# Edge network: inverse deviations from a ScalarE square root and one VectorE reciprocal, in place of Newton steps on VectorE

## The chip, the cores and the metric

The kernel runs on one core of one Trainium2 chip. The metric is device time in microseconds (us). Before the change it is 17780.12 us, the median of 3 runs (17768.55 to 17810.48).

## The reference, cut to what matters

Four graph layers run one after another on 6250 nodes of 64 features and 206250 edges that are sorted by destination. The change is in the second one, the edge network with four heads. For head h and every edge:

```python
alpha = concat([q_i * K_v[src], q_i * K_E], axis=1) * scale   # 128 features
gate  = sigmoid(_ln(alpha, ln_g[h], ln_b[h]))
m     = concat([V_v[src], V_E], axis=1)
m     = (m @ Wu[h] + bu[h]) * gate
m     = leaky(_ln(m @ Wm[h] + bm[h], mln_g[h], mln_b[h]))     # 64 features
heads.append(segment_sum(m, dst))
```

where `_ln(x, g, b)` is `(x - mean) * rsqrt(var + 1e-5) * g + b` over the features. Each edge and head therefore needs two inverse deviations: one of alpha (128 features) and one of m @ Wm + bm (64 features).

## The kernel before, in words

Edges lie on the 128 partitions. A tile is 128 edges, a group is G = 4 tiles, and there are NG = 404 groups. With H = 4 heads a group has Q = G * H = 16 pairs of tile and head, so one step needs 16 inverse deviations of alpha and 16 of the output: a vector of 32 elements on each partition. Every stage over the edges is a loop over groups. The helper `steps` writes the first steps out, then a hardware loop whose body holds U = 4 groups, then the last steps.

The edge network's loop is `sweep1`, written once for each engine, as a pipeline in which step i works on several groups at a time:

- GpSimd gathers the rows of source and destination nodes (L1096), and for an older group multiplies and adds the affine vectors mg and mb (L1118, L1121).
- TensorE transposes the rows (L932), makes K_E (`edge_k`, L939), transposes the normalised alpha of group i-1 head by head (`turn`, L947), makes V @ Wu (`m_u`, L954), then of group i-2 the product with Wm (`o_pair`, L964 and L966), and of group i-4 the scatter by a one-hot matrix (`sums`, L977). The order is written out by hand: turn and m_u of heads 0 to 3, with edge_k, o_pair and sums between.
- ScalarE takes in step i, in this order: `norm` of head 1, sigmoid(0), norm of head 2, a copy, sigmoid(1), norm of head 3, sigmoid(2), take_o(0), sigmoid(3), norm(i, 0), take_o(1). `norm` (L781) is four ACTIVATEs with scale `rstd` and bias `shift`. `sigmoid(h)` (L787) waits for turn(h) and for gate_m(h - 2), since there are two gate buffers. `take_o` (L794, L795) squares and copies the output of o_pair.
- VectorE makes alpha (L550, and `edge_half` L523) and its statistics (L529). `gate_m(h)` (L535) multiplies the value by the gate of head h. Then comes the chain of small steps (L585 to L609), in which each `settle` waits for the step before it. Then the one-hot (L399), the normalised output y (L618), and `add` (L406), which adds the scattered sums to the accumulator; adds 0 and 1 take those of sums(0), adds 2 and 3 those of sums(1).

The chain holds 19 small steps (CH = 19). The first eight make the two variances, `var[0:16]` and `var[16:32]`. L600 makes a first guess of the inverse root by arithmetic on the bits, and L603, L605 and L607 refine it three times. L609 makes the shift. On VectorE gate_m(1) stands ahead of the chain and gate_m(2) behind it. On TensorE m_u(3) waits for gate_m(1), and sums(1) waits for adds 0 and 1. Everything on one engine is done in program order, and engines wait for each other by semaphores: chain1 counts the small steps, gated the sigmoids, gm_ready the gate_m, o_taken the take_o, normed the norms.

Elsewhere in the kernel square roots are made on ScalarE by the helper `root` (L761), followed by a reciprocal on VectorE (L367, L744).

Of the kernel before, what the change touches and what calls it, by code (L numbers as in the profile page):

```python
# [26 lines left out]
P = 128  # L27
# [26 lines left out]
MAGIC = float(0x5F3759DF)  # L54
# [21 lines left out]
def gnn(nc, a, out):  # L76
    ctx = ExitStack()
    with ctx:
# [126 lines left out]
        tmp = [view(2 * G * H, [2 * G * H]) for _ in range(5)]  # L205
# [73 lines left out]
        chain1 = sem("chain1")  # L279
        normed = sem("normed")  # L280
# [13 lines left out]
        CH = 19  # L294
# [44 lines left out]
        def _(dve):  # L339
# [166 lines left out]
            for s in range(2):  # L506
                link(V.memset(o_sq[s], 1.0), mark="sweep1")
# [5 lines left out]
            def sweep1(i, k, s, inside):  # L513
# [50 lines left out]
                if now[1]:  # L564
                    gate_m(1)
# [15 lines left out]
                var, u, d2, sm, m2 = tmp  # L581
                root = rstd[z]
                if now[2]:
                    dve.wait_ge(normed, Q * (i - 1))
                small_step(V.tensor_tensor(d2[:, 0:Q], st[:, :, 1], st[:, :, 4], ALU.subtract))  # L585
                small_step(V.tensor_tensor(sm[:, 0:Q], st[:, :, 1], st[:, :, 4], ALU.add))
                small_step(V.tensor_tensor(m2[:, 0:Q], st[:, :, 2], st[:, :, 5], ALU.add))
                small_step(V.tensor_reduce(var[:, Q:2 * Q], o_sq[odd], AX, ALU.add))  # L588
                settle()

                small_step(V.scalar_tensor_tensor(d2[:, 0:Q], d2[:, 0:Q], P / 4.0, d2[:, 0:Q],
                                                  ALU.mult, ALU.mult))
# [19 lines left out]
                if now[1]:  # L612
                    gate_m(2)
# [139 lines left out]
        def _(act):  # L753
# [18 lines left out]
            def sweep1(i, k, s, inside):  # L772
# [40 lines left out]
                if now[1]:  # L813
                    sigmoid(3)
# [3 lines left out]
                if now[2]:  # L818
                    take_o(1)
# [478 lines left out]
```

## Time and profile before

| | |
|---|---|
| median of 3 runs | 17780.12 us (17768.55 to 17810.48) |
| profiled execution | 17803.45 us |
| its span | 17801.3 us |
| mean granted TensorE clock | 0.738 |
| edge network's sweep, 2959 to 11520 us | 8561 us, 404 groups |
| PE busy in the sweep | 7228.05 us |
| DVE busy in the sweep | 7069.66 us |
| ACT busy in the sweep | 4760.21 us |
| POOL busy in the sweep | 5741.32 us |

The profile is of one execution. PE is TensorE, DVE VectorE, ACT ScalarE and POOL GpSimd. "Lnnn" is a line of the kernel before. A timeline's row gives the start in us, the duration in us, the engine, the line, the operation, its tiles, how many instructions are merged in the row, and in brackets the idle time before it with what ended it. The granted clock is a share of TensorE's full clock.

### The profile page before, as it was taken

The page shows a single profiled execution, that of the slowest core. Times are in us where ns is not written, and L with a number is a line of the kernel's source. Part 1 is how long each engine was busy: PE and PEld are TensorE (multiplying, and loading weights), DVE is VectorE, ACT ScalarE, POOL GpSimd, SP SyncE. Part 2 cuts the span into 40 slices and gives each one's busy share as a digit, 9 for nine tenths or more (in the row PEclk, how much of TensorE's full clock was granted, in tenths as well). Part 3 has the DMA queues.
Part 4 walks back from the last instruction along what each step waited for, and adds up shares of the span by engine and source line. Part 5 has one row for each costly group of instructions (what it writes and reads, how often), then busy time and mean ns, then how long its engine had stood idle before and what let it go on. Part 6 is the DMA issues. An engine that isn't in the chain of part 4 may idle for free.

```text
span 17801.3 us, 231614 instructions
## 1 busy us (share of the span) xinstructions
PE 11205.7 (63%) x52461; PEld 8279.5 (47%) x52462; DVE 10797.0 (61%) x29437; ACT 5021.6 (28%) x10532; POOL 10715.0 (60%) x10914
## 2 busy tenths in 40 slices
PE   5333335888888888888888888733333355555565
PEld 4222223666666565656566656522222233333454
DVE  7222225888888888888888888732222333333776
ACT  0000002555555555555555555400000011111000
POOL 0666664666666666666666666556666566666000
PEclk9999998888888888888888888755555555555555
DMA  0000002222222222222222222100000111111111
GB/s 25 22 22 22 22 22 70 62 63 64 61 62 63 64 62 62 62 62 62 62 62 62 62 63 64 42 22 22 22 22 22 29 46 46 46 46 46 51 48 40
DMA packets 474914, 838.02 MB, mean 47 GB/s; under 512 B 151155, under 2 KB 264980, under 8 KB 472725
## 3 DMA queue, kind: packets, MB, share of 16 engines
q0 software_dynamic: 310272, 637.61, 13.3%
q1 hardware_dynamic: 164116, 195.98, 3.6%
q14 instruction: 511, 4.19, 0.1%
q8 instruction: 15, 0.25, 0.0%
HBM read 755.78 MB, written 77.21 MB: 47 GB/s over the span
## 4 chain that ended last, share of the span: by engine, by line
DVE 30%; issue 27%; POOL 24%; PE 13%; DVEq 4%; POOLq 1%; ACT 1%; DMA 0%; SPq 0%; ACTq 0%
POOL arena L1096 22%; DVE acc L406 5%; DVE arena L529 4%; PE psum L977 4%; DVE arena L618 2%; DVE arena L588 2%; PE psum L939 2%; DVE arena L523 2%; PE psum L954 2%; DVE arena L561 2%; PE psum L947 2%; DVEq L329 1%; POOL idx_src L1103 1%; DVE arena L607 1%; DVE arena L603 1%
## 5 line engine op out<-in xcount | busy, mean ns | idle before, releaser
L1096 POOL DMA_INDIRECT arena<-table,idx_src x6464 | 6216.8, 962 | 4461.7 <-DVE arena L523 1803.1
L406 DVE TENSOR_TENSOR acc<-acc,psum 64x128 f32 (+2 forms) x6464 | 2041.1, 316 | 4230.0 <-PE psum L904 3019.2
L904 PE MATMUL psum<-arena 128*64 128x128 f32 x6464 | 1585.9, 427 | 3274.3 <-DMA arena<-table,idx_src 3274.3
L904 PEld LDWEIGHTS psum<-arena 128*64 128x64 f32 x6464 | 1266.1, 223 | 3593.9 <-issue 3569.1
L781 ACT ACTIVATE arena<-arena 128x128 f32<-128x128 f32 x6464 | 2648.8, 483 | 620.2 <-DVE arena L609 620.2
L1096 POOL DMA_INDIRECT arena<-table1q,idx_dst x1616 | 1873.1, 1159 | 492.3 <-issue 492.3
L787 ACT ACTIVATE arena<-psum,cols 128x512 f32<-128x512 f32 x1616 | 1256.1, 777 | 3047.8 <-PE psum L947 3044.6
L964 PEld LDWEIGHTS psum<-wm,arena 128*128 128x128 f32 x12928 | 1742.0, 202 | 560.2 <-issue 464.4
L954 PE MATMUL psum<-arena,wvu 128*128 128x512 f32 x3232 | 1966.9, 695 | 1.4 <-DVE arena L535 1.4
L964 PE MATMUL psum<-wm,arena 128*128 128x64 f32 x12928 | 1797.5, 285 | 0.1
L761 ACT ACTIVATE small<-small 128x49 f32<-128x49 f32 (+1 forms) x7 | 1.6, 233 | 6252.5 <-DVE small L365 3716.9
L977 PE MATMUL psum<-arena 128*128 128x128 f32 x6464 | 1140.3, 333 | 980.6 <-DVE acc L406 974.7
L977 PEld LDWEIGHTS psum<-arena 128*128 128x128 f32 x6464 | 1040.0, 237 | 1266.8 <-DVE acc L406 753.8
L939 PE MATMUL psum<-ke,arena 64*128 64x256 f32 x3232 | 1228.7, 514 | 341.3 <-DVE arena L523 341.3
L529 DVE BATCH_NORM_STATS2 arena<-arena 128x6 f32<-128x128 f32 x6464 | 1329.0, 279 | 118.6 <-DVE arena L523 45.3
L673 DVE TENSOR_TENSOR arena<-psum,arena 128x512 f32<-128x512 f32 x404 | 279.4, 692 | 1571.5 <-PE psum L1047 1571.5
L535 DVE SCALAR_TENSOR_TENSOR arena<-psum,cols,arena 128x512 f32<-128x512 f32 x1616 | 1198.9, 742 | 48.1 <-PE psum L954 43.7
L1121 POOL TENSOR_TENSOR arena<-arena,mb 128x1024 f32<-128x1024 f32 x404 | 1198.4, 2966 | 31.7
L947 PE MATMUL psum<-ident,arena 128*128 128x128 f32 x6464 | 1200.1, 315 | 5.7 <-ACT arena L781 5.7
L939 PEld LDWEIGHTS psum<-ke,arena 64*128 64x128 f32 x3232 | 722.5, 248 | 1015.3 <-DVE arena L523 608.3
L399 DVE TENSOR_TENSOR arena<-rel,iota_f 128x512 f32<-128x512 f32 x1616 | 1108.6, 686 | 96.4 <-issue 91.0
L1039 PE MATMUL psum<-ident,arena 128*64 128x128 f32 x1616 | 417.4, 414 | 1158.1 <-DMA arena<-table,idx_src 1158.1
(171 smaller groups left out, 14815.5 us busy)
## 6 DMA issues: line engine op xcount, KB each, us to landing
arena<-table,idx_src POOLq DMA_INDIRECT x6464, 2.4
kept_rows<-arena SPq DMA_DIRECT2D x404, 132.0 KB, 1.7
arena<-kept_rows SPq DMA_DIRECT2D x404, 132.0 KB, 2.1
arena<-in_edge_t SPq DMA_DIRECT2D x404, 128.0 KB, 2.8
arena<-table1q,idx_dst POOLq DMA_INDIRECT x1616
table<-arena SPq DMA_DIRECT2D x7, 1120.0 KB, 4.2
table1q<-arena SPq DMA_DIRECT2D x7, 896.0 KB, 6.4
table<-arena SPq DMA_DIRECT2D x2, 1568.0 KB, 5.1
```

The lines of the kernel that those rows point to most:

```text
L406: V.tensor_tensor(at_, at_, sums, ALU.add).then_inc(added, 1)
L529: V.bn_stats(st[:, n, :], alpha[z][:, n // H, n % H, :, :].rearrange("p a d -> p (a d)")).then_inc(stats1, 1)
L535: V.scalar_tensor_tensor(gm[odd][:, h, :, :].rearrange("p t n -> p (t n)"), psum[:, 4 + h % 2, :], cols[:, 0, h:h + 1], gate[:, h % 2, :], ...
L781: A.activation(at_, at_, ACT.Identity, bias=shift[z][:, n:n + 1], scale=rstd[z][:, n:n + 1]).then_inc(normed, 1)
L787: A.activation(gate[:, h % 2, :], psum[:, 2 + h % 2, :], ACT.Sigmoid, bias=cols[:, 2, h:h + 1], scale=cols[:, 1, h:h + 1]).then_inc(gated, 1)
L904: last = M.matmul(psum[0:D, z, t * WIN:(t + 1) * WIN], rows[s][:, t, :], onehot[z][:, t, :], start=True, stop=True)
L939: last = M.matmul(psum[:, 1, t * H * D:(t + 1) * H * D], xt[s][D:P, 2 * j + t, :], ke[D:P, :], start=True, stop=True)
L947: last = M.transpose(psum[:, 2 + h % 2, t * P:(t + 1) * P], alpha[odd][:, t, h, :, :].rearrange("p a d -> p (a d)"), ident[:, :])
L954: M.matmul(psum[:, 4 + h % 2, :], wvu[:, h, :], xt[prev].rearrange("p t n -> p (t n)"), start=True, stop=True).then_inc(m_done, 1)
L964: M.matmul(psum[:, 6, at_ + h * D:at_ + (h + 1) * D], gm[z][:, h, 2 * j + t, :], wm[:, h, :], start=h == 0, stop=False)
L977: last = M.matmul(psum[:, 7, at_:at_ + WIN], msg[z][:, t * H + 2 * half:t * H + 2 * half + 2, :].rearrange("p h d -> p (h d)"), onehot[z][ ...
L1096: K.indirect_dma_start(out=dst[:, t, :], out_offset=None, in_=table, in_offset=bass.IndirectOffsetOnAxis(ap=idx[:, t:t + 1], axis=0)).then ...
```

## The change

VectorE's chain loses the scaling of the variances, the first guess and the nine refining steps. The raw variances go to ScalarE, which makes their deviations by two ACTIVATEs with Sqrt (scale 1/128 and 1/64, bias from a new small tile `eps`), into a new tile `deviation`, and signals `rooted`. VectorE waits for that, takes one reciprocal of 32 elements, and makes the shift. The chain has 8 small steps now. gate_m(1) moves from ahead of the chain to behind its first six steps, gate_m(2) follows it, and both stand ahead of the wait for `rooted`. On ScalarE the square roots stand behind sigmoid(3), and take_o(1) moves from behind norm(i, 0) to ahead of it. Sigmoid and Sqrt are in different activation tables, so each step has two table loads.

```diff
-        tmp = [view(2 * G * H, [2 * G * H]) for _ in range(5)]
+        var, deviation = (view(2 * G * H, [2 * G * H]) for _ in range(2))
+        d2, sm, m2 = (view(G * H, [G * H]) for _ in range(3))
+        eps = view(2, [2])
...
-        CH = 19
+        CH = 8
...
+            link(V.memset(eps[:, 0:1], EPS1))
+            link(V.memset(eps[:, 1:2], EPS), mark="sweep1")
...
                 if now[0]:
                     edge_half(1)
-                if now[1]:
-                    gate_m(1)
...
+                small_step(V.tensor_tensor(d2, st[:, :, 1], st[:, :, 4], ALU.subtract))
+                small_step(V.tensor_tensor(sm, st[:, :, 1], st[:, :, 4], ALU.add))
+                small_step(V.tensor_tensor(m2, st[:, :, 2], st[:, :, 5], ALU.add))
+                after(dve, rooted, i)
+                small_step(V.tensor_reduce(var[:, Q:2 * Q], o_sq[odd], AX, ALU.add))
+                settle()
+                small_step(V.scalar_tensor_tensor(d2, d2, P / 4.0, d2, ALU.mult, ALU.mult))
+                settle()
+                small_step(V.tensor_tensor(var[:, 0:Q], d2, m2, ALU.add))
+                if now[1]:
+                    gate_m(1)
+                    gate_m(2)
                 if now[2]:
                     dve.wait_ge(normed, Q * (i - 1))
...
+                dve.wait_ge(rooted, i + 1)
+                small_step(V.reciprocal(root, deviation))
                 settle()
-                small_step(V.scalar_tensor_tensor(var[:, 0:Q], d2[:, 0:Q], P * EPS1, m2[:, 0:Q],
-                                                  ALU.add, ALU.add))
-                settle()
-                small_step(V.tensor_scalar(var[:, 0:Q], var[:, 0:Q], 1.0 / P, None, ALU.mult))
-                small_step(V.tensor_scalar(var[:, Q:2 * Q], var[:, Q:2 * Q], 1.0 / D, EPS, ALU.mult, ALU.add))
-                settle()
-                small_step(V.tensor_scalar(root.bitcast(I32), var.bitcast(I32), -0.5, MAGIC, ALU.mult, ALU.add))
-                for _ in range(3):
-                    settle()
-                    small_step(V.scalar_tensor_tensor(u, root, -0.5, root, ALU.mult, ALU.mult))
-                    settle()
-                    small_step(V.tensor_tensor(u, u, var, ALU.mult))
-                    settle()
-                    small_step(V.scalar_tensor_tensor(root, u, 1.5, root, ALU.add, ALU.mult))
-                settle()
-                small_step(V.scalar_tensor_tensor(shift[z], sm[:, 0:Q], -0.5, root[:, 0:Q], ALU.mult, ALU.mult))
-                if now[1]:
-                    gate_m(2)
+                small_step(V.scalar_tensor_tensor(shift[z], sm, -0.5, root[:, 0:Q], ALU.mult, ALU.mult))
+                settle()
...
                 if now[1]:
                     sigmoid(3)
+                act.wait_ge(chain1, CH * (i + 1) - 2)
+                Q = G * H
+                A.activation(deviation[:, 0:Q], var[:, 0:Q], ACT.Sqrt, bias=eps[:, 0:1], scale=1.0 / P)
+                A.activation(deviation[:, Q:2 * Q], var[:, Q:2 * Q], ACT.Sqrt, bias=eps[:, 1:2], scale=1.0 / D
+                             ).then_inc(rooted, 1)
+                if now[2]:
+                    take_o(1)
                 if now[0]:
                     act.wait_ge(chain1, CH * (i + 1))
                     norm(i, z, 0)
-                if now[2]:
-                    take_o(1)
-            steps(act, sweep1, NG, 4, 2)
+            steps(act, sweep1, NG, 4, 4)
```

## Rows read from the trace of the kernel before

**Rows 1.** The page, part 1: busy time, share of the span, instructions, by engine.
```profile
PE 11205.7 (63%) x52461; PEld 8279.5 (47%) x52462; DVE 10797.0 (61%) x29437; ACT 5021.6 (28%) x10532; POOL 10715.0 (60%) x10914
```

**Rows 2.** Windows, the edge network's sweep: length, busy by engine, clock, DMA share, GB/s.
```profile
2959.00:11520.00 8561.00, 7228.05 (x35549) 5153.79 (x35550) 7069.66 (x19872) 4760.21 (x10101) 5741.32 (x4840) 0.82 0.21 62
```

**Rows 3.** Waits in the sweep: total us, times, the longest; ACT, then PE.
```profile
ACT arena L787 <- PE psum L947: 3044.6, 1530, 5.8
ACT arena L781 <- DVE arena L609: 620.2, 298, 14.4
...
PE psum L977 <- DVE acc L406: 974.7, 364, 5.3
```

**Rows 4.** Timeline of DVE in the group at 6010 us.
```profile
6008.60 1.65 DVE L529 BATCH_NORM_STATS2 arena<-arena 128x6 f32<-128x128 f32 x8
6010.16 0.74 DVE L535 SCALAR_TENSOR_TENSOR arena<-psum,cols,arena 128x512 f32<-128x512 f32 x1
6010.81 0.18 DVE L585 TENSOR_TENSOR arena<-arena 128x16 f32<-128x16 f32 x1
...
6012.56 0.17 DVE L594 SCALAR_TENSOR_TENSOR arena<-arena 128x16 f32<-128x16 f32 x1
6012.77 0.17 DVE L597 TENSOR_SCALAR arena<-arena 128x16 f32<-128x16 f32 x1
...
6015.32 0.17 DVE L609 SCALAR_TENSOR_TENSOR arena<-arena 128x16 f32<-128x16 f32 x1
...
6016.17 0.68 DVE L399 TENSOR_TENSOR arena<-rel,iota_f 128x512 f32<-128x512 f32 x1
```

**Rows 5.** Timeline of ACT in the same group: sigmoid(3).
```profile
6012.29 0.78 ACT L787 ACTIVATE arena<-psum,cols 128x512 f32<-128x512 f32 x1 [0.43 <-PE psum L947]
```

**Rows 6.** Timeline of PE in the same group: end of o_pair(1), then sums(1).
```profile
6015.13 0.28 PE L966 MATMUL psum<-bm_parts,ones 3*128 3x256 bf16 x1
6018.93 2.08 PE L977 MATMUL psum<-arena 128*128 128x128 f32 x8 [3.52 <-DVE acc L406]
```

**Rows 7.** Timeline of ACT around two of its five table loads.
```profile
2977.25 1.28 ACT L787 ACT_TABLE_LOAD   x1
2978.54 0.78 ACT L787 ACTIVATE arena<-psum,cols 128x512 f32<-128x512 f32 x1
...
16569.31 1.28 ACT L761 ACT_TABLE_LOAD   x1
```

**Rows 8.** Line 761, the square roots: shortest, median and longest in ns.
```profile
L761 ACT ACTIVATE small<-small x7: 203/245/246, 2841.9 to 17735.5; 128x49 f32<-128x49 f32 x5, 64x1 f32<-64x1 f32 x2
```

**Rows 9.** Groups of DVE by form, reciprocals: busy us, mean ns, idle before.
```profile
L367 DVE RECIPROCAL dn<-small 128x49 f32<-128x49 f32 x4 | 1.9, 465 | 1.5 <-ACT small L761 1.5
L744 DVE RECIPROCAL small<-small 128x7 f32<-128x7 f32 x7 | 1.4, 201 | 0.2
```

**Rows 10.** Timelines of ACT, DVE and PE in a second group, at 5634 us.
```profile
5634.48 0.78 ACT L787 ACTIVATE arena<-psum,cols 128x512 f32<-128x512 f32 x1 [0.43 <-PE psum L947]
...
5636.99 0.68 DVE L399 TENSOR_TENSOR arena<-rel,iota_f 128x512 f32<-128x512 f32 x1
...
5639.91 1.47 PE L977 MATMUL psum<-arena 128*128 128x128 f32 x8 [2.31 <-DVE acc L406]
```

**Rows 11.** Timelines of ACT and DVE in a third group, at 5150 us.
```profile
5150.10 0.78 ACT L787 ACTIVATE arena<-psum,cols 128x512 f32<-128x512 f32 x1 [0.44 <-PE psum L947]
...
5151.25 0.68 DVE L399 TENSOR_TENSOR arena<-rel,iota_f 128x512 f32<-128x512 f32 x1
```

**Rows 12.** Timelines of ACT and DVE in a fourth group, at 5494 us.
```profile
5494.00 0.78 ACT L787 ACTIVATE arena<-psum,cols 128x512 f32<-128x512 f32 x1 [2.46 <-PE psum L947]
...
5492.16 0.68 DVE L399 TENSOR_TENSOR arena<-rel,iota_f 128x512 f32<-128x512 f32 x1
```

**Rows 13.** Timeline of PE: two sums(1) in a row, one group apart.
```profile
5497.04 1.16 PE L977 MATMUL psum<-arena 128*128 128x128 f32 x8
...
5516.02 2.08 PE L977 MATMUL psum<-arena 128*128 128x128 f32 x8 [3.71 <-DVE acc L406]
```

More of the change, by code:

```diff
@@ L53 @@
 BIG = 1.0e30
-MAGIC = float(0x5F3759DF)
 assert NC == NB * BC and HI * LO == NP and T % (2 * HG) == 0
@@ L279, in gnn @@
         chain1 = sem("chain1")
+        rooted = sem("rooted")
         normed = sem("normed")
@@ L506, in _ @@
             for s in range(2):
-                link(V.memset(o_sq[s], 1.0), mark="sweep1")
+                link(V.memset(o_sq[s], 1.0))
+            link(V.memset(eps[:, 0:1], EPS1))
+            link(V.memset(eps[:, 1:2], EPS), mark="sweep1")
             Q = G * H
@@ L580, in sweep1 @@
                     dve.wait_ge(o_taken, 2 * (i - 2))
-                var, u, d2, sm, m2 = tmp
                 root = rstd[z]
+                small_step(V.tensor_tensor(d2, st[:, :, 1], st[:, :, 4], ALU.subtract))
[3 more added lines that the diff above has]
+                small_step(V.tensor_reduce(var[:, Q:2 * Q], o_sq[odd], AX, ALU.add))
@@ L583, in sweep1 @@
+                settle()
+                small_step(V.scalar_tensor_tensor(d2, d2, P / 4.0, d2, ALU.mult, ALU.mult))
+                settle()
+                small_step(V.tensor_tensor(var[:, 0:Q], d2, m2, ALU.add))
+                assert n[0] == CH - 2
+                if now[1]:
+                    gate_m(1)
+                    gate_m(2)
                 if now[2]:
                     dve.wait_ge(normed, Q * (i - 1))
-                small_step(V.tensor_tensor(d2[:, 0:Q], st[:, :, 1], st[:, :, 4], ALU.subtract))
@@ L586, in sweep1 @@
-                small_step(V.tensor_tensor(sm[:, 0:Q], st[:, :, 1], st[:, :, 4], ALU.add))
-                small_step(V.tensor_tensor(m2[:, 0:Q], st[:, :, 2], st[:, :, 5], ALU.add))
-                small_step(V.tensor_reduce(var[:, Q:2 * Q], o_sq[odd], AX, ALU.add))
+                dve.wait_ge(rooted, i + 1)
+                small_step(V.reciprocal(root, deviation))
                 settle()
-                small_step(V.scalar_tensor_tensor(d2[:, 0:Q], d2[:, 0:Q], P / 4.0, d2[:, 0:Q],
-                                                  ALU.mult, ALU.mult))
+                small_step(V.scalar_tensor_tensor(shift[z], sm, -0.5, root[:, 0:Q], ALU.mult, ALU.mult))
@@ L593, in sweep1 @@
+                assert n[0] == CH
                 settle()
-                small_step(V.scalar_tensor_tensor(var[:, 0:Q], d2[:, 0:Q], P * EPS1, m2[:, 0:Q],
-                                                  ALU.add, ALU.add))
-                settle()
-                small_step(V.tensor_scalar(var[:, 0:Q], var[:, 0:Q], 1.0 / P, None, ALU.mult))
-                small_step(V.tensor_scalar(var[:, Q:2 * Q], var[:, Q:2 * Q], 1.0 / D, EPS, ALU.mult, ALU.add))
-                settle()
-                small_step(V.tensor_scalar(root.bitcast(I32), var.bitcast(I32), -0.5, MAGIC, ALU.mult, ALU.add))
@@ L610, in sweep1 @@
-                assert n[0] == CH
-                if now[1]:
-                    gate_m(2)
                 c = C2 * (i - 3)
```

## The prediction

> **What bounds the kernel now.** I read the page's shares first [rows 1], then the windows cut at the edge network's sweep [rows 2], then the waits inside it [rows 3], then the timelines of single groups [rows 4 to 6, 10, 11]. The sweep holds 8561 of the 17801.3 us and runs 404 groups, so a group takes 21.19 us on average. In it TensorE is busy 84%, VectorE 83%, ScalarE 56% [rows 2]. The two full engines take turns: TensorE waits for VectorE's additions 974.7 us in 364 groups, 2.7 us each [rows 3], and its granted clock is 0.82 of full, a mix of its two levels, 2.4 and 1.2 GHz. The diff touches this sweep only, so everything is priced there, per group, times 404.
>
> The point where a shift of time becomes a shift of the end is the one-hot at L399: from its start to the second pair of scatter matmuls (L977) it is 18.93 - 16.17 = 2.76 us [rows 4, 6], and there both engines meet again, once in every group. What moves L399 moves the group.
>
> **VectorE's own part.** Before, gate_m(1) (L535), then the chain L585 to L609, then gate_m(2) and L399. In the group at 6010 the twelve steps that go (L597, L598, L600, nine Newton steps) take 15.32 - 12.77 = 2.55 us [rows 4]. One reciprocal of 128x32 comes in. The trace has 128x7 at 0.20 and 128x49 at 0.465 [rows 9]; by width 0.36, plus 0.04 until a dependent step starts (L594 ends at 12.73, L597 starts at 12.77). The shift step stays, and a settle of 0.04 now stands behind it. Alone this is -2.55 + 0.44 = -2.11 us a group, -852 us over the sweep. That is the lower bound of the change, and it holds only if the new wait for ScalarE costs nothing.
>
> **What the new wait costs.** Three things now follow in series. VectorE does gate_m(1) after the first six steps. ScalarE's sigmoid(3) waits for gate_m(1), because it overwrites the gate buffer that gate_m(1) reads. Behind sigmoid(3) come the table load, both square roots and the hand-over. Prices:
> - table load 1.28 us, started 0.02 after the instruction before it, next ACTIVATE 0.01 behind it [rows 7];
> - two square roots of 128x16: the nearest rows are 0.20 for 64x1 and 0.245 for 128x49 [rows 8]. I take 0.50 for the pair, since these have another operand and end in sequence; below 0.32, above 1.4 (two sigmoids of 128x512 overlapped, 0.78 each [rows 5]);
> - hand-over between the engines 0.04, estimated from the step gap above; not over 0.3.
>
> From the end of sigmoid(3) to the reciprocal that is 0.02 + 1.28 + 0.01 + 0.50 + 0.04 = 1.85 us; reciprocal, shift and settles are 0.36 + 0.04 + 0.17 + 0.04 = 0.61. So L399 starts 0.78 + 1.85 + 0.61 = 3.24 us after the start of sigmoid(3).
>
> The Trainium skill, page "ScalarE: Activation LUTs", section "What ACT_TABLE_LOAD costs", gives a switch 1283 ns of load and about 1380 ns of drain, 2.66 us in all. The trace has the 1283 ns and no drain: the sigmoid starts 0.01 us behind the load [rows 7]. By the page the switch to the square root would put 404 x 1.38 = 557 us more on the path; that is a rival below.
>
> **Three kinds of group.** Which one a group is depends on how late TensorE brings the fourth transpose to sigmoid(3).
> - Early, as at 6012. Statistics end at 6010.25. The chain starts at 10.29, L594 at 10.29 + 1.75 = 12.04, gate_m(1) at 12.13 (0.09 is how far independent steps overlap), ending 12.87. Sigmoid(3), ready at 12.29 [rows 5], is pushed to 12.91, and L399 comes at 12.91 + 3.24 = 6016.15 against 6016.17: -0.02. The 2.11 us saved are spent waiting.
> - Middle, as at 5634. Sigmoid(3) starts at 34.48 as before; L399 at 5637.72 against 5636.99 [rows 10]: +0.73.
> - Late, as at 5150. Sigmoid(3) at 50.10; L399 at 5153.34 against 5151.25 [rows 11]: +2.09. Here the old chain was over before sigmoid(3) ended and needed nothing of ScalarE; the new one can't start its tail until TensorE's transpose and the load are through. In the worst example, sigmoid(3) at 94.00 and L399 at 92.16, it is 97.24: +5.08 [rows 12].
>
> How many of each follows from one row: ScalarE idled for L609 in 298 groups, 620.2 us in all [rows 3]. That idle is 2.4 us in an early group (sigmoid(3) ends at 13.07, L609 at 15.49) and 1.1 in the middle one; with 2.5 and 1.1, 2.5x + 1.1(298 - x) = 620.2 gives x = 209 early and 89 middle. The other 106 did not wait and are late. For their mean price I take 2.5, near the ordinary 2.09, with one in seven like the worst. Sum: 209 x (-0.02) + 89 x 0.73 + 106 x 2.5 = -4 + 65 + 265 = **+326 us**.
>
> **What is covered.** The load back to the sigmoid set: a load stands ahead of the wait of its ACTIVATE (at 16569.31 it runs directly behind the Exp, over 1100 us before the root it serves, the last at 17735.5 [rows 7, 8]), so it falls into ScalarE's idle before the next sigmoid(0), part of 3044.6 us in 1530 waits, 2 us each [rows 3]; without that cover it costs 1.28 on gate_m(0), at most 517 us. take_o(1) goes ahead of norm(i, 0), and its matmuls end 3.1 us after sigmoid(3) starts (15.41 against 12.29 [rows 5, 6]), about when the square roots are through, so it adds no wait; norm(i, 0) comes later by take_o's two ACTIVATEs, and TensorE needs it only in the next step. ScalarE has 21.19 - 4760 / 404 = 9.4 idle us a group [rows 2] for 3.1 us of new work; I cost all this at nothing. TensorE's m_u(3) is held by gate_m(1) for as long as sigmoid(3) is pushed, 0.6 us in an early group, where TensorE has 3.52 us idle behind it [rows 6]. Queued behind VectorE's new wait are the reciprocal, L399, y, the additions and gate_m(3); for these wait TensorE's scatter matmuls, and that is the priced path. The two memsets of eps, the moved wait for normed and ScalarE's two more tail steps cost under 5 us together. No DMA is added or moved; GpSimd is busy 67% of the sweep [rows 2] and its gathers start from edge_half(1), ahead of all this.
>
> **TensorE's clock.** The eight matmuls of sums(1) take 2.08 us after 3.52 us of idle [rows 6], 1.47 after 2.31 [rows 10], and 1.16 after none [rows 13]; I read the first as the low level throughout, the last as the full one and the middle one as a change on the way. Afterwards L977 always starts 3.24 + 2.76 = 6.0 us behind sigmoid(3), its forerunners end 3.1 us behind it, so every group has 2.7 to 2.9 us of idle. Before it was 3.5, 2.3 or none by kind, with the mean of 2.7 from above. The mean stays, so I keep the mix of clocks and put the two ways it could turn among the rivals.
>
> **The sum.** 17801.3 + 326 = 18127 us of span, 18129.6 for the profiled execution (17803.45). The median of the three runs, 17780.12, is 23.3 below that, so the prediction is 18106 us, +1.8%.
>
> **Rivals.**
> 1. More late groups. Idle before L977 in every group costs the full clock in those that had it, and a low clock makes the next sigmoid(3) late. With 200 late groups and 204 at the mean of the others, 61 / 298 = 0.20: 500 + 42 = +542, 18322 us. For: the 3.52 and 3.71 us of idle shown both end in matmuls of 2.08 us [rows 6, 13]. Against: the mean idle stays, and early groups had 3.5 us before and get less.
> 2. Faster, by the clock. The idle of 2.8 us leaves the clock up in most groups, TensorE is early, all groups become early ones, and each saves part of what a full-clock group has: 5516.02 - 5497.04 = 18.98 us [rows 13] against 21.19. Half of the 2.2 us in half of the groups, and no late ones: 404 x 0.55 = -222, 17558 us. It decides if idle of 2.8 us counts as short. Against: the middle group's 2.3 us already ended in a slower start.
> 3. Break-even: the early pattern everywhere with the clock unchanged, because VectorE's waiting lets TensorE catch up. 404 x (-0.02) = -8, 17772 us. For: both engines meet anew in each group. Against: lateness comes from TensorE's own low-clock work, which VectorE's waiting does not shorten.
> 4. The drain of 1.38 us comes with each load in the loop: +326 + 557, 18663 us. The load in the trace speaks against it.
> 5. The change does as it says and ScalarE hides it all: -852, 16928 us. Only if sigmoid(3) did not stand ahead of the load.
>
> **Chances.** Forecast 0.58 (own range 17950 to 18260), rival 1 0.18, rival 2 0.08, rival 3 0.09, rival 4 0.05, rival 5 0.02. The range leaves out rivals 2, 4 and 5 and reaches over 3 and 1; for the square roots at their upper price (0.9 us in 404 groups, 364 us) it goes to some 18460, and below to 17690. 0.2% (36 us) is what can be told from no change. Rival 3 I split in halves between same and slower or faster; faster 0.08 + 0.02 + 0.03 = 0.13, same 0.05, slower 0.82.
>
> **What would show it.** Right: VectorE idle of 1.5 to 2 us before the reciprocal in early groups and 3 to 4 in late ones, released by the square root; two loads of 1.28 us a group; L399 about 3.2 us behind sigmoid(3) in every group; idle before L977 of 2.6 to 3 us everywhere; 21.9 to 22.1 us a group. Wrong: sigmoid(3) starting before gate_m(1) ends, a reciprocal that waits for nothing, a gap behind the load, or a group time below 21.1 us with a granted clock well over 0.82.

## The result: 4.6% slower

The changed kernel takes 18608.2 us (median of four, 18572.2 to 18634.5), the kernel before, run beside it, 17788.5: ratio 1.046, 95% interval 1.044 to 1.048, 820 us more. Forecast was 18106 with a range up to 18460. The direction is right; the size is more than twice the +326 us of the sum, and the time lies above the range. The profiled execution has a span of 18570.4 us, 769 more than before, and a granted clock of 0.732 over the whole span.

The page of the kernel after, part 1, answers to [rows 1]:

```profile
PE 11587.3 (62%) x52461; PEld 8534.8 (46%) x52462; DVE 10258.4 (55%) x24951; ACT 6232.0 (34%) x12154; POOL 10450.6 (56%) x10914
```

VectorE lost 539 us of work. The steps that went are 12 of 0.17 us, one reciprocal of 0.35 came, which makes 404 x 1.69 = 683 us less; part of it went back into the alpha product (L550 before, L554 now), which takes 1.91 us instead of 1.58 in the mean. ScalarE gained 1210 (two loads and two small ACTIVATEs a group: 404 x (2.57 + 0.50) = 1240). TensorE has the same instructions and 382 us more busy time: the low clock holds for 9.0 us of a group instead of 7.4. The windows of the sweep, as [rows 2], then its waits (total us, times, longest), as [rows 3]:

```profile
2959.00:12310.00 9351.00, 7622.40 (x35576) 5410.35 (x35575) 6534.80 (x15370) 5973.60 (x11724) 5465.52 (x4823) 0.81 0.19 57
```

```profile
PE psum L975 <- DVE acc L408: 1205.5, 403, 3.8
...
DVE arena L601 <- ACT arena L811: 1111.8, 407, 4.5
```

By the windows' round edges the sweep is 790 us longer than in [rows 2]; the whole change lies in it. The new wait for the root (L601 for L811) costs VectorE 1111.8 us, 2.7 a group, which is more than the 2.11 a group that the missing Newton steps saved. The one-hot (L399 before, L401 now) comes later, and TensorE waits for the additions in every group (1205.5 in 403) instead of in 364.

Timelines of one ordinary group, the one that answers to [rows 4 to 6]: VectorE, ScalarE, TensorE (start, duration, then in brackets the idle before and what ended it).

```profile
6014.57 1.41 DVE L539 SCALAR_TENSOR_TENSOR arena<-psum,cols,arena 128x512 f32<-128x512 f32 x2
6018.12 0.35 DVE L601 RECIPROCAL arena<-arena 128x32 f32<-128x32 f32 x1 [2.13 <-ACT arena L811]
6018.51 0.17 DVE L603 SCALAR_TENSOR_TENSOR arena<-arena 128x16 f32<-128x16 f32 x1
6018.81 0.69 DVE L401 TENSOR_TENSOR arena<-rel,iota_f 128x512 f32<-128x512 f32 x1
```

```profile
6005.19 1.28 ACT L780 ACT_TABLE_LOAD   x1 [3.51 <-PE psum L945]
6006.49 0.78 ACT L780 ACTIVATE arena<-psum,cols 128x512 f32<-128x512 f32 x1
...
6015.42 0.78 ACT L780 ACTIVATE arena<-psum,cols 128x512 f32<-128x512 f32 x1 [1.39 <-DVE arena L539]
6016.22 1.28 ACT L810 ACT_TABLE_LOAD   x1
6017.51 0.31 ACT L810 ACTIVATE arena<-arena 128x16 f32<-128x16 f32 x1
6017.72 0.29 ACT L811 ACTIVATE arena<-arena 128x16 f32<-128x16 f32 x1
```

```profile
6018.58 0.28 PE L964 MATMUL psum<-bm_parts,ones 3*128 3x256 bf16 x1
...
6021.58 2.08 PE L975 MATMUL psum<-arena 128*128 128x128 f32 x8 [2.72 <-DVE acc L408]
```

The series is the predicted one: gate_m(1) ends, sigmoid(3) starts at 6015.42, load, two roots that end at 6018.01, reciprocal at 6018.12, one-hot at 6018.81, which is 3.39 behind sigmoid(3) (forecast 3.24), and sums(1) 2.77 later (forecast 2.76). Its 2.72 us of idle is in the forecast's 2.6 to 3.

So an ordinary group is no surprise. Measured from one sums(1) to the next over some 394 groups, the mean went from 21.12 to 23.07 us, but not evenly: 328 groups have a mean of 21.9, in the forecast's 21.9 to 22.1, and 66 groups take 26 us or more, 28.90 in the mean. Before there was none. They all stand at one place: the hardware loop's body holds four groups, and these are the ones in which the loop turns. The kernel before takes longer there too, 22.99 us against 20.50 in the other three. So a long group costs 28.90 - 22.99 = 5.91 us, and the 66 make 390 of the 769 us; the remaining 379 us are spread over all other groups and are about the forecast sum of 326. Two further executions of the same kernel have 71 and 65 such groups.

One of them, TensorE's timeline from one sums(1) to the next, then windows cut between them (columns as in [rows 2]; the clock is the third number from the end), then VectorE's timeline:

```profile
5585.72 2.05 PE L975 MATMUL psum<-arena 128*128 128x128 f32 x8 [3.56 <-DVE acc L408]
...
5594.06 2.07 PE L937 MATMUL psum<-ke,arena 64*128 64x256 f32 x4 [0.69 <-DVE arena L527]
...
5614.60 1.80 PE L975 MATMUL psum<-arena 128*128 128x128 f32 x8 [3.16 <-DVE acc L408]
```

```profile
5585.70:5589.00 3.30, 3.28 (x13) 2.81 (x14) 1.38 (x3) 0.66 (x2) 3.22 (x2) 0.50 0.00 0
5589.00:5596.00 7.00, 6.31 (x14) 3.13 (x13) 3.71 (x11) 4.08 (x7) 0.75 (x3) 0.50 0.01 2
5596.00:5603.00 7.00, 7.00 (x26) 5.21 (x25) 6.50 (x18) 2.32 (x5) 1.96 (x2) 0.50 0.09 25
5603.00:5607.00 4.00, 4.00 (x14) 2.97 (x14) 0.75 (x1) 1.75 (x3) 2.87 (x4) 0.50 0.44 123
```

```profile
5592.18 1.22 DVE L554 TENSOR_TENSOR arena<-arena 128x1024 f32<-128x1024 f32 x1 [3.24 <-PE psum L945]
...
5611.03 0.35 DVE L601 RECIPROCAL arena<-arena 128x32 f32<-128x32 f32 x1 [4.46 <-ACT arena L811]
```

sums(1) starts after 3.56 us of idle at 1.2 GHz (0.50). Then TensorE idles once more, 0.69 us at edge_k, and is granted 0.50 for over 21 us, though from 5596 to 5607 it has no gap at all. Its low-clock work brings the transpose for sigmoid(3) late, VectorE waits 4.46 us for the root, and the group takes 28.88.

Two things about the turn are not new. VectorE stands idle for 3.25 us ahead of the alpha product there, before and after the change alike, and for 0.24 to 0.66 us in the other groups. (The row above names a matmul for it, but in 44 of 99 such groups before the change the profile names no releaser.) And 12 of the 98 groups at the turn were already at the low clock for over 20 us before the change. What is new is how many there are and what each costs: before, such a group took 25.8 us instead of 22.6, 3.1 more; now 66 take 28.9 instead of 23.6, 5.3 more. In the kernel with loads that nothing waits for (below) 34 groups stay low for over 20 us and cost only 2.4 more each.

### The profile page after: what moved, and what is told of

It reads as the page before. It is cut to its first block, busy times and chain, and to the rows that moved or that the text cites. A ratio compares the mean times of both kernels' runs of the same rounds, so it can differ in the third digit from the quotient of the medians.

```text
span 18570.4 us, 225494 instructions
## 1 busy us (share of the span) xinstructions
PE 11587.3 (62%) x52461; PEld 8534.8 (46%) x52462; DVE 10258.4 (55%) x24951; ACT 6232.0 (34%) x12154; POOL 10450.6 (56%) x10914
## 4 chain that ended last, share of the span: by engine, by line
issue 25%; DVE 24%; POOL 24%; PE 17%; ACT 4%; DVEq 3%; POOLq 1%; DMA 0%; ACTq 0%; SPq 0%
POOL arena L1094 22%; PE psum L975 5%; DVE acc L408 4%; DVE arena L533 4%; ACT L810 3%; PE psum L952 3%; DVE arena L611 3%; PE psum L937 2%; PE psum L945 2%; PE psum L962 2%; DVE arena L527 2%; DVE arena L539 2%; DVE arena L588 2%; DVE arena L565 2%; DVEq L331 1%
## 5 line engine op out<-in xcount | busy, mean ns | idle before, releaser
L774 ACT ACTIVATE arena<-arena 128x128 f32<-128x128 f32 x6464 | 2609.0, 486 | 1.3 <-DVE arena L603 1.3
L975 PE MATMUL psum<-arena 128*128 128x128 f32 x6464 | 1281.9, 363 | 1211.1 <-DVE acc L408 1205.5
L1094 POOL DMA_INDIRECT arena<-table1q,idx_dst x1616 | 1618.4, 1001 | 492.7 <-issue 492.7
L975 PEld LDWEIGHTS psum<-arena 128*128 128x128 f32 x6464 | 1166.4, 264 | 1514.6 <-DVE acc L408 918.3
L937 PE MATMUL psum<-ke,arena 64*128 64x256 f32 x3232 | 1281.2, 532 | 225.5 <-DVE arena L527 225.5
L1116 POOL TENSOR_TENSOR arena<-arena,mg 128x1024 f32<-128x1024 f32 x404 | 956.4, 2367 | 452.6 <-DVE arena L611 447.7
L937 PEld LDWEIGHTS psum<-ke,arena 64*128 64x128 f32 x3232 | 761.7, 261 | 941.6 <-DVE arena L527 564.9
L401 DVE TENSOR_TENSOR arena<-rel,iota_f 128x512 f32<-128x512 f32 x1616 | 1111.2, 688 | 149.9 <-issue 79.5
```

Of the source, the lines that this page charges most:

```text
L774: A.activation(at_, at_, ACT.Identity, bias=shift[z][:, n:n + 1], scale=rstd[z][:, n:n + 1]).then_inc(normed, 1)
L937: last = M.matmul(psum[:, 1, t * H * D:(t + 1) * H * D], xt[s][D:P, 2 * j + t, :], ke[D:P, :], start=True, stop=True)
L975: last = M.matmul(psum[:, 7, at_:at_ + WIN], msg[z][:, t * H + 2 * half:t * H + 2 * half + 2, :].rearrange("p h d -> p (h d)"), onehot[z][ ...
L1094: K.indirect_dma_start(out=dst[:, t, :], out_offset=None, in_=table, in_offset=bass.IndirectOffsetOnAxis(ap=idx[:, t:t + 1], axis=0)).then ...
```

## The experiments

What had to be told apart: is it the load in series behind sigmoid(3) and the clock that follows, the two loads as such, the load back to the sigmoid set, the place of gate_m(1), or something that the changed order does to VectorE and GpSimd. Means per group below are taken as above. Five studies ran, each beside its own kernel before. In the second and fourth that one took 17763.3 and 17767.4 us, in the fifth 17741.5; in the first and third, called the late studies below, 18396.0 and 18412.1 (last section). Gains in us are differences within one study.

**The changed kernel again**, as the base of the second and fourth study.

> The changed kernel as it is, so that the kernels of these studies can be set against it and the kernel before on one chip. In the first study the kernel before took 18396 us where it had taken 17788, and TensorE's semaphores came 3 to 5 us behind the recorded ends of its matmuls in a fifth of the cases, where they came 0.01 us behind in the two first profiles. If the change costs the same everywhere: 1.046 of the kernel before. If what slows TensorE there also meets the new serial path (sigmoid(3), load, roots, reciprocal): 1.06 to 1.08. Against that value the kernel without loads (1.0455 of before in the first study) is to be read: equal would mean that the loads cost nothing.

> The changed kernel as the reference of this study. On a chip where the kernel before takes about 17770 us: 1.046 to 1.050 of it. On one where it takes about 18400 us, where TensorE's semaphores come late in a fifth of the cases, it has not been run yet; the kernel without loads took 1.0455 there, so 1.06 to 1.09.

18636.9 us, 1.0495 (1.0471 to 1.052), and 18604.2, 1.0472 (1.0454 to 1.0489). Neither was in a late study, so what the change costs there was not measured.

**No loads.** The two small ACTIVATEs stay in place and use Identity, which needs no table load; the square root is left out of the computation.

```diff
-A.activation(deviation[:, 0:Q], var[:, 0:Q], ACT.Sqrt, ...
-A.activation(deviation[:, Q:2 * Q], var[:, Q:2 * Q], ACT.Sqrt, ...
+A.activation(deviation[:, 0:Q], var[:, 0:Q], ACT.Identity, ...
+A.activation(deviation[:, Q:2 * Q], var[:, Q:2 * Q], ACT.Identity, ...
```

> The changed kernel with Identity in place of Sqrt in the two small ACTIVATEs (this leaves the square root out of the computation); Identity is served by the table that the sigmoids use, so both table loads of a group go, and all waits and the order stay. Theory A: the loads themselves, each 1.28 us on the path (one behind sigmoid(3), one behind the wait of sigmoid(0)), are what turned the saving of 2.1 us a group on VectorE into a loss; then this falls below the kernel before, to 17200 to 17600 us. Theory B: the new order (gate_m(1) behind the chain, VectorE waiting for ScalarE, the steadier idle of TensorE and its lower clock) costs by itself and the loads little; then it stays at 18200 us or more.

> The kernel without loads again (Identity in place of Sqrt, which leaves the square root out). Theory A, the loads on the path cost 1.28 us each for every group: 0.03 to 0.05 below the changed kernel of the same study. Theory B, order and clock: within 0.01 of it.

In the second study 17764.5 us, 0.9994 (0.9982 to 1.0007): 872 less than the changed kernel beside it, about as theory A says there, and no faster than before, where theory A had hoped for 17200 to 17600. (In the late first study 1.0455, 1.0425 to 1.0485.) Windows, then waits, of the run with 0.9994:

```profile
2959.00:11500.00 8541.00, 7142.23 (x35558) 5071.56 (x35558) 6548.57 (x15351) 4919.66 (x10908) 5506.48 (x4820) 0.86 0.21 62
```

```profile
DVE arena L601 <- ACT arena L811: 529.0, 402, 3.1
PE psum L975 <- DVE acc L408: 626.1, 394, 2.2
```

Taking the loads out takes back the whole loss in this study. Of the 872, 404 x 1.28 = 517 is the load's own length in the series; some 350 more come with it. TensorE's idle before sums(1) fell from 3.0 to 1.57 us, the time at the low clock from 9.3 to 5.8 us a group, and 20 groups instead of 71 take 26 us or more (26.8 in the mean, not 28.9). Even free of loads the new series gains nothing: VectorE still waits 529 us for ScalarE. In the late first study this kernel, without any load, stood at 1.0455, so there the series behind sigmoid(3) costs by itself.

**Both loads, off the path.** The kernel before, with a two-element square root behind sigmoid(3), which nothing waits for.

```diff
 sigmoid(3)
+A.activation(spare[:, 0:2], spare[:, 2:4], ACT.Sqrt)
```

> The kernel before with one added ACTIVATE of Sqrt on two spare elements behind sigmoid(3), for which nothing waits: the two table loads of a group without the rest of the change. Forecast of the prediction (both covered by ScalarE's idle): 17760 to 17830 us. Theory A: the load back starts only once the transpose for sigmoid(0) is there, so sigmoid(0) comes 1.28 us later in every group; gate_m(0) has about 1.4 us of slack where TensorE is early and none where it is late, so 17900 to 18200 us.

> The kernel before with the two loads of a group alone, again. The kernel with the preloaded sigmoid table was as slow as the changed one (18626 against 18637), so the load behind the wait for the transpose costs nothing there. If that holds here: 17740 to 17800 us. If the load matters as long as nothing else is in the way: 17850 to 18100 us.

> The kernel before with the two loads of a group alone, for which nothing waits. It took 1.007 and 1.006 of the kernel before on the two chips where TensorE is late. If loads off the path are covered by ScalarE's idle, also where TensorE is on time: 1.000 to 1.003. If they cost through sigmoid(0): 1.005 to 1.02. In no case the 1.05 of the changed kernel, if that comes from the load in the path to the reciprocal.

1.0033 (1.0021 to 1.0044), 17831.1 against 17767.4; in the late studies 1.0071 (1.0054 to 1.0088) and 1.0057 (1.0032 to 1.0081). Its loads by group of instructions (count, busy us, mean ns, idle before and what ended it):

```profile
L789 ACT ACT_TABLE_LOAD x404 | 518.3, 1283 | 1526.8 <-PE psum L950 1524.3
...
L817 ACT ACT_TABLE_LOAD x404 | 518.3, 1283 | 7.4
```

1037 us of loads cost 64 where no one waits for the root. One of the two, L789, even starts behind a wait and not ahead of it.

**The roots ahead of sigmoid(3).** The wait for the chain and both roots move up one step.

```diff
-                if now[1]:
-                    sigmoid(3)
                 act.wait_ge(chain1, CH * (i + 1) - 2)
 ...
                              ).then_inc(rooted, 1)
+                if now[1]:
+                    sigmoid(3)
```

> The changed kernel with the two square roots ahead of sigmoid(3) on ScalarE instead of behind it. The load of the square root's table then falls into the time in which VectorE still makes the variances, and the load back falls before sigmoid(3), whose gate VectorE needs some 5 us later. Theory A: neither load is on the path any more, L401 comes about 1.5 us earlier than in the kernel before in a group where TensorE is early, and the time is 17100 to 17600 us. Theory B: TensorE's lateness and clock rule, and sigmoid(2) is then what the roots wait behind; 17800 to 18300 us.

> The kernel with both square roots ahead of sigmoid(3) again, hoped for on a chip where TensorE's semaphores follow its matmuls at once. Theory A (the load of the root's table behind sigmoid(3) is what costs): L401 no longer waits for the fourth transpose, only for the third (sigmoid(2)), take_o(0), one load and the roots; 17300 to 17550 us where the kernel before takes 17763. Theory B (moving the roots only moves the wait, since sigmoid(2) is late as well when TensorE is): 17750 to 18000 us.

> The kernel with both roots ahead of sigmoid(3). It took 1.007 and 1.008 of the kernel before on the two chips where TensorE is late. Theory A (the root's load behind sigmoid(3) is the cause of the loss): on a chip where TensorE is on time at most the time of before, 17300 to 17700 us; anywhere, 0.03 or more below the changed kernel. Theory B (the roots' wait moves to sigmoid(2) and stays as long): within 0.01 of the changed kernel.

17796.7 us, 1.0015 (1.0003 to 1.0027), 808 less than the changed kernel beside it; in the late studies 1.0069 (1.0046 to 1.0091) and 1.0078 (1.0053 to 1.0103). Theory A holds in its difference (0.046 below the changed kernel), not in its hope of a gain (17300 to 17700). ScalarE in an ordinary group, and the sweep's waits:

```profile
5999.74 1.28 ACT L808 ACT_TABLE_LOAD   x1
6001.04 0.31 ACT L808 ACTIVATE arena<-arena 128x16 f32<-128x16 f32 x1
...
6001.56 1.28 ACT L780 ACT_TABLE_LOAD   x1
6002.86 0.78 ACT L780 ACTIVATE arena<-psum,cols 128x512 f32<-128x512 f32 x1
```

```profile
DVE arena L601 <- ACT arena L809: 381.0, 261, 2.4
PE psum L975 <- DVE acc L408: 444.0, 350, 2.4
```

The same work, loads and arithmetic, costs 837 us or 29 by one place in ScalarE's order (18604.2 and 17796.7 against 17767.4). The root has stopped waiting for gate_m(1) and for TensorE's fourth transpose. What is left: the load back now stands ahead of sigmoid(3), and the idle before sums(1) is 1.13 us. In the late first study the place weighs more than the loads: with both loads and the roots ahead of sigmoid(3) 1.0069, without loads and the roots behind it 1.0455.

**gate_m(1) ahead of the chain again**, as before the change.

```diff
                     edge_half(1)
+                if now[1]:
+                    gate_m(1)
 ...
-                    gate_m(1)
                     gate_m(2)
```

> The changed kernel with gate_m(1) back ahead of the chain, as it stood before. Sigmoid(3) then no longer waits for the chain where TensorE is early, the 1.39 us of ScalarE's wait for gate_m(1) go, and m_u(3) starts 1 us sooner; the chain starts 0.65 us later, which the load hides. Expected: 0.3 to 0.8 us less in the half of the groups where TensorE is early, 100 to 250 us less than the changed kernel. If TensorE's lateness rules in nearly all groups: no difference.

18321.7 us, 1.0311 (1.0293 to 1.0329), 315 less than the changed kernel beside it and more than expected. Sigmoid(3) no longer waits for a gate_m that waits for six chain steps. By the forecast's series it would start 12.91 - 12.29 = 0.62 us earlier in 209 early groups, 130 us. The traces show the gain elsewhere: the three groups of the loop's body without the turn take 21.7 us in the mean in both kernels, and the one with the turn falls from 27.3 to 24.9. The groups of 26 us or more fell from 71 to 31, while the low clock holds for 9.3 us a group in both: less of it stands in one piece.

**The load back, ahead of its wait.** A two-element sigmoid directly behind the previous step's work loads the set early.

```diff
                     norm(i - 1, odd, 1)
+                    A.activation(spare, eps, ACT.Sigmoid)
                     sigmoid(0)
```

> The changed kernel with one Sigmoid ACTIVATE on two spare elements between norm(i-1, 1) and sigmoid(0), so that the load back runs in ScalarE's idle and not behind the wait for the transpose. Theory A: sigmoid(0) starts 1.28 us sooner in every group, and 0.3 to 1 us of that reaches the end, since gate_m(0) has some 1.4 us of slack where TensorE is early: 100 to 400 us less than the changed kernel. If the load back was covered all the same, as the prediction costed it: no difference (within 40 us).

18626.5 us, 1.0483 (1.0466 to 1.0501); the changed kernel beside it 1.0495, so no difference. ScalarE:

```profile
6007.28 1.28 ACT L793 ACT_TABLE_LOAD   x1
...
6011.20 0.78 ACT L781 ACTIVATE arena<-psum,cols 128x512 f32<-128x512 f32 x1 [2.42 <-PE psum L947]
```

The load is 1.28 us earlier against its wait, sigmoid(0) starts 5.42 instead of 6.69 us behind sums(1), and the end does not move: TensorE and VectorE have other work until the step's end.

**TensorE kept busy ahead of sums(1)** in the changed kernel: three more matmuls, timed to fill the idle. Their product is thrown away.

```diff
                     o_pair(1)
+                if now[0] and now[4]:
+                    after(pe, alpha_e, 2 * i + 2)
+                    for _ in range(3):
+                        M.matmul(psum[:, 1, 0:2 * P], ident[:, :], ...
```

> The changed kernel with three matmuls of 128x256 (about 1.3 us at the full clock, results not used) between o_pair(1) and sums(1), in TensorE's idle of 2.7 us. Theory C: the idle of 2.7 us in every group takes the clock down, above all through the group behind the loop's turn, where it stays down for 22 us and the group takes 28.9 instead of 23.5 us (about 66 groups, some 350 us); the fill keeps it up, and the time falls to 18150 to 18350 us with a granted clock of 0.75 or more. If the clock is only a follower: 18600 to 18800 us.

> The changed kernel with three matmuls of 128x256 in TensorE's idle ahead of sums(1), again. In the changed kernel of the second study that idle was 3.0 us a group and the low clock held for 9.3 of 23.2 us; in the kernel without loads 1.57 us, and 5.8 of 21.1 us. Theory C (the loads cost 1.28 us each way on the path and as much again by the clock that the longer idle takes down): the fill brings the clock back and the time to 18150 to 18350 us. If the clock is only a follower: 18600 us or more.

> The changed kernel with the fill in TensorE's idle. It took 1.033 and 1.034 of the kernel before on the two chips where TensorE is late. Theory C (the longer idle takes the clock down, and this doubles what the load costs): 200 to 400 us less than the changed kernel in the same study. If the clock is a follower: not below it.

18772.4 us, 1.0569 (1.055 to 1.0589), 168 more than the changed kernel beside it, where theory C had 200 to 400 less. (In the late studies 1.0345, 1.0321 to 1.037, and 1.0334, 1.0305 to 1.0364, with nothing beside it to set it against.) Windows of the whole sweep and of the middle of a group, then the timelines of TensorE and, of one row, VectorE:

```profile
3100.00:12400.00 9300.00, 7627.35 (x37135) 5485.06 (x37134) 6542.17 (x15011) 5867.27 (x11457) 5362.43 (x4728) 0.87 0.19 56
...
6010.50:6020.70 10.20, 10.20 (x36) 7.45 (x35) 7.67 (x20) 4.06 (x8) 5.28 (x6) 0.51 0.25 68
```

```profile
6001.52 1.13 PE L975 MATMUL psum<-arena 128*128 128x128 f32 x8 [2.11 <-DVE acc L408]
...
6008.98 1.13 PE L937 MATMUL psum<-ke,arena 64*128 64x256 f32 x4 [3.39 <-DVE arena L527]
6010.54 1.83 PE L952 MATMUL psum<-arena,wvu 128*128 128x512 f32 x2
...
6024.50 1.56 PE L1006 MATMUL psum<-wu,ident 128*128 128x256 f32 x6
6027.72 1.16 PE L975 MATMUL psum<-arena 128*128 128x128 f32 x8 [1.66 <-DVE acc L408]
```

```profile
6007.10 1.23 DVE L554 TENSOR_TENSOR arena<-arena 128x1024 f32<-128x1024 f32 x1 [3.27 <-issue]
```

The fill works at its place: sums(1) takes 1.13 and 1.16 us, full clock, and the sweep's granted clock rises from 0.81 to 0.87. But the gap has moved. The group shown is one at the loop's turn: VectorE stands idle for its 3.27 us there, TensorE, early now, waits 3.39 us for edge_half behind it and is then at 0.51 for ten microseconds, in front of the last transpose, which sigmoid(3) and with it the whole series wait for. Low-clock time fell to 6.2 us a group, and yet 129 groups take 26 us or more (26.9 in the mean), 40 of them at the turn, and the time rose. "More clock is less time" has fallen; which work is done at the low clock seems to decide, which the fill suggests and does not show.

**The roots one place further up, and GpSimd's order.** First the roots directly behind sigmoid(2), ahead of take_o(0) too; then the same with GpSimd's multiplication (affine) issued between its two gathers; then that order alone in the kernel before.

```diff
                     sigmoid(2)
+                act.wait_ge(chain1, CH * (i + 1) - 2)
+ ...
-                    gather(q[s].rearrange(...), table1q, idx_dst[s], q_in[s])
                 if inside or g >= 5:
                     affine(g - 5, 1 - s)
+                if inside or g < NG:
+                    gather(q[s].rearrange(...), table1q, idx_dst[s], q_in[s])
```

> As the last, with the roots also ahead of take_o(0), directly behind sigmoid(2). The roots then wait for the load alone in groups where TensorE is late: up to 0.95 us sooner there. Where TensorE is early the roots wait for the variances, and take_o(0) and with it o_pair(1) come 0.7 us later, into TensorE's idle. Expected: 50 to 200 us less than the last one, if theory A holds; no difference if VectorE alone sets the pace by then.

> The kernel with both roots directly behind sigmoid(2) (1.004 of before on a chip where TensorE is late, where roots ahead of sigmoid(3) alone had 1.008 and on the other kind 1.0015), and on GpSimd the affine step between the gather by source and the gather by destination instead of behind both. In the kernel with roots ahead of sigmoid(3) VectorE's L554 takes 2.23 us where 1.22 is its time alone, since GpSimd's affine step on 128x1024 runs beside it. If that is the reason why 2.1 us less work on VectorE gives no faster kernel: L554 falls to 1.2 to 1.5 us and the ratio to 0.96 to 0.985. If the affine step only collides with another operation instead: 0.995 to 1.01.

> The kernel before with the same order on GpSimd alone. L554 takes 1.59 us there, 0.37 over its time alone. If the collision is what it costs: 0.992 to 0.998 of before. If it now waits for y (the affine step needs the y of the same step) and the gather by destination comes late: 1.00 to 1.02. Against the last kernel it tells how much of a gain belongs to GpSimd's order and how much to the roots.

The first alone, in the late third study: 1.0041 (1.0026 to 1.0055), 76 us less than the roots ahead of sigmoid(3) beside it. Both: **17098.7 us, 0.9638 (0.9622 to 0.9654)**, 643 us faster than the kernel before beside it, and the best of all. GpSimd's order alone: 1.0031 (1.0018 to 1.0043). The sweep's windows and waits in the fastest, and the alpha product (L554) in it (count, busy us, mean ns, idle before):

```profile
2959.00:10880.00 7921.00, 6716.66 (x35577) 4781.41 (x35575) 6508.14 (x15346) 5950.94 (x11696) 5479.75 (x4808) 0.91 0.23 67
```

```profile
DVE arena L601 <- ACT arena L806: 86.1, 156, 1.1
PE psum L975 <- DVE acc L408: 152.5, 267, 3.8
```

```profile
L554 DVE TENSOR_TENSOR arena<-arena 128x1024 f32<-128x1024 f32 x401 | 754.5, 1881 | 442.6 <-issue 411.5 <-PE psum L945 30.8
```

VectorE waits 86 us for the roots instead of 1112, TensorE 153 for the additions instead of 1206, idle before sums(1) is 0.36 us, low-clock time 3.2 us a group, and no group takes 26. The time lies in the forecast's range, but by luck, since its reason failed. That was a collision: in the changed kernel the alpha product takes 1.23 us in the 100 cases in which no tensor operation of GpSimd overlaps it and 2.14 in the 302 others. It was to fall to 1.2 to 1.5 us in the mean, and it stays at 1.88 (1.91 in the changed kernel). What carries the gain is open: GpSimd's order alone gives none in the kernel before, and the roots directly behind sigmoid(2) alone ran only in a late study, so the roots' place and the two together are not told apart.

## Why the prediction was right and wrong

- **VectorE's own part, right.** 2.55 us of steps went, one reciprocal of 0.35 came (forecast 0.36).
- **The series behind sigmoid(3), right in kind, 0.27 us short in size.** Load 1.28, no gap behind it, roots 0.31 and 0.29 overlapped to 0.50, as forecast. The Trainium skill's page "ScalarE: Activation LUTs", "What ACT_TABLE_LOAD costs", gives 1283 ns and some 1380 ns of drain a switch; the 808 loads have the first and not the second, and rival 4 fell. In the mean the one-hot comes 3.51 us behind sigmoid(3), not 3.24: 0.11 of hand-over instead of 0.04, 0.13 to 0.24 for the last settle instead of 0.04, and in one group of the loop's four the reciprocal starts 0.46 us behind the roots, for a reason that the traces do not tell. 404 x 0.27 = 109 us.
- **Statistics, a term left out.** They end 0.56 us later behind sums(1) (12.75 against 12.19 us), and so does all behind them; the alpha product's 0.3 us and TensorE's lower clock lie ahead of it. I had priced VectorE's first half as unchanged. By stretches, a group's +1.95 us is +0.56 to the end of the statistics, +0.56 from there to sigmoid(3) (3.43 to 3.99), +0.93 to the one-hot (2.58 to 3.51) and -0.11 to sums(1) (2.92 to 2.81); the forecast had a price for the last two and, by kind of group, part of the second.
- **gate_m(1), mis-sized and misplaced.** The forecast's series has it at 130 us, in the early groups; undoing the move alone gives 315, at the loop's turn.
- **The back-load, wrong in its place, right in its price.** Forecast: it runs ahead of the wait of its ACTIVATE. It starts after the 3.51 us of waiting. Sigmoid(0) has two waits: the first is an instruction by itself, ahead of the load; only a last one rides on the ACTIVATE, behind it. (The root has one wait, and its load does run ahead of it.) The preload shows that the 1.28 us cost nothing.
- **The clock and the start of sigmoid(3), the step that failed.** "The mean stays, so I keep the mix of clocks." With this the forecast took sigmoid(3) from the trace of before and moved it only for gate_m(1), by 0.62 us in 209 of 404 groups, 0.32 in the mean. It moved by 1.12. In the three groups of the loop's body without the turn it starts 15.37 us behind sums(1) instead of 14.95, which is 0.42 and near the forecast; at the turn 20.90 instead of 17.64, which is 3.26, and 101 x 3.26 = 329 us. In the sweep the mean clock did nearly stay, 0.82 to 0.81. But idle of 2.7 to 3.6 us now stands ahead of sums(1) in every group, so that 394 of 395 sums(1) take over 1.3 us (1.16 at the full clock), against 232 before, and behind the loop's turn, where VectorE's own 3.25 us of idle follow, TensorE stays low for over 20 us in 66 groups instead of 12. These 66 are 390 of the 769 us. Rival 1, with a chance of 0.18, names this mechanism ("a low clock makes the next sigmoid(3) late") and gives it 18322, since its late groups cost 2.5 us each; the 66 cost 5.9. Its worst example [rows 12], +5.08, was the better model; it is one of the 12. The idle of 3.71 in front of 2.08 us of matmuls [rows 13] was read and not carried on. The forecast had no price for the turn, where the kernel before too takes 2.5 us longer.
- **Rivals 2, 3 and 5** each took it that the clock or ScalarE would give the wait back. At the forecast's place of the roots it did not; at their early places it did, where the root does not stand behind the wait for the fourth transpose.

That the load in series behind sigmoid(3) is the cause is shown from both sides where the kernel before takes 17.8 ms (no loads, -872 us; loads with no one waiting, +64; same loads one step earlier, -808). In the late first study the series without a load was slow as well (1.0455), so what stands ahead of the roots is as much a part of the cause as the load. That the rest beyond 517 us goes through the low clock is argued from counts (71 and 20 long groups) and not shown by switching the clock itself: the one try at it, the fill, moved the gap.

## What to carry to other kernels

When work moves to another engine, look at what stands ahead of it in that engine's order: here the whole change costs 837 us with its two square roots behind an instruction that waits for TensorE and 29 us with them ahead of it. Price a new stall on TensorE twice, for its length and for the low clock that its later work then has, and ask which of that work the next wait hangs on; an average clock does not tell. The groups at a loop's turn, where stalls add up, want a price of their own: here they are one in four and hold more than half of the loss.

## What the hardware showed

- Late studies. The kernel before takes 17741 to 17789 us beside the result and in the second, fourth and fifth study, 18396 and 18412 in the first and third. In the traces of the late ones many of TensorE's completions reach the waiting engine well behind the recorded end of the matmuls; in the kernel without loads of the first study 17% of those of the transposes come over 1 us late (3.7 in the median) and 47% of those of o_pair (4.1), and some completions are missing from the record. In the other studies it is 0.01 us. ScalarE, and its waits, in that kernel ("remote" stands where the profile finds no instruction of this core that ended close to the completion):

```profile
6020.18 0.60 ACT L787 ACTIVATE arena<-psum 128x512 f32<-128x512 f32 x1 [3.51 <-remote]
```

```profile
ACT arena L787 <- remote: 1112.0, 256, 7.8
ACT arena L780 <- remote: 835.8, 204, 6.8
```

  The first waits for this matmul on TensorE, which ended at 6015.80:

```profile
6015.52 0.28 PE L964 MATMUL psum<-bm_parts,ones 3*128 3x256 bf16 x1
```

  The same kernel is 1.0455 there and 0.9994 in the second study: a variant must be judged beside a run of the kernel before in its own study, and even the ratio need not carry over. Why the studies differ is open. The recorded expectations speak of two kinds of chip, but the first and the fourth study, one late and one not, carry the same chip number, 3, so that is not shown.
- TensorE was granted 1.2 GHz through 11 us in which the profile shows no gap (5596 to 5607), behind a stall of 3.56 us at sums(1) and one of 0.69 at edge_k.
- A long stretch at the low clock has no fixed price. Groups at the loop's turn that are low for over 20 us take 3.1 us more than the others there in the kernel before (12 groups), 2.4 with loads that nothing waits for (34) and 5.3 in the changed kernel (66), where the roots stand behind TensorE's last transpose.
- Of 1037 us of table loads, all but 64 could be hidden.
